# Two-layer attention with expert layers on one core: x kept on chip between the layers, expert outputs written by plain indirect writes, routing steps moved by an iteration or two

## The reference, cut to what matters

```python
x = x + tanh(g_xattn[0]) * attention_0(layernorm(x), ctx, mask)      # 64 x 64 tokens of 128, 16 heads of 8
x = x + tanh(g_ffn[0])   * experts_0(layernorm(x))                   # 8 experts, hidden 512, gelu, top 1
x = x + tanh(g_xattn[1]) * attention_1(layernorm(x), ctx)
x = x + tanh(g_ffn[1])   * experts_1(layernorm(x))                   # 16 experts, hidden 64, silu, top 2, capacity 8
```

## Time and profile before

| | us |
|---|---|
| median of 3 runs (lowest to highest) | 517.33 (516.51 to 517.77) |
| the profiled execution | 514.45 |
| its span, first to last instruction | 512.4 |
| PE busy | 443.6 |
| DVE busy | 349.9 |
| ACT busy | 320.6 |
| POOL busy | 272.6 |

### The profile page before, as it was taken

The page is one execution under the profiler, slowest core; times in us unless marked ns, Lnnn a source line. Parts: engine busy times, 40 slices in busy tenths (PEclk is TensorE's granted clock), DMA queues, the critical chain, the costliest instruction groups (busy, mean ns, idle before and its releaser), DMA issues.

```text
span 512.4 us, 21949 instructions
## 1 busy us (share of the span) xinstructions
PE 443.6 (87%) x8481; PEld 324.1 (63%) x8481; DVE 349.9 (68%) x883; ACT 320.6 (63%) x764; POOL 272.6 (53%) x325
## 2 busy tenths in 40 slices
PE   2789999999988796999998799998998697779996
PEld 1456676666655685999973466666665565445554
DVE  5578778888768665545532678888898677644545
ACT  2355566666865873677744466777777377685653
POOL 2622634646466178888886445553545236534454
PEclk9999999999999998999999799999999899898999
DMA  7124444232111155565436000110031000000112
GB/s 209 51 55 130 98 127 125 82 95 70 44 55 35 35 139 90 82 89 71 44 35 155 2 25 24 45 35 24 4 95 26 21 4 3 2 2 5 42 53 68
DMA packets 50629, 30.69 MB, mean 60 GB/s; under 512 B 12384, under 2 KB 46944, under 8 KB 50528
## 3 DMA queue, kind: packets, MB, share of 16 engines
q1 hardware_dynamic: 37072, 18.54, 13.7%
q0 software_dynamic: 6640, 4.67, 7.2%
q10 hardware_dynamic: 6816, 6.08, 4.3%
HBM read 19.42 MB, written 9.85 MB: 57 GB/s over the span
## 4 chain that ended last, share of the span: by engine, by line
PE 49%; DVE 20%; issue 13%; ACT 7%; POOL 4%; DMA 3%; ACTq 1%; DVEq 1%; SPq 0%; POOLq 0%
PE T_ps L865 8%; DVE maxes L600 7%; PE S_ps L854 6%; DVE prob L608 4%; PE A_ps L880 4%; PE f_H_ps L1199 3%; PE m_H_ps L1458 3%; PE f_Y_ps L1213 3%; PE S_ps L848 3%; PE Q_ps L835 2%; PE m_X_ps L1485 2%; PE m_T_ps L1498 2%; PE Q_ps L747 2%; PE m_X_ps L1469 2%; PE X_ps L897 2%
## 5 line engine op out<-in xcount | busy, mean ns | idle before, releaser
L600 DVE TENSOR_REDUCE maxes<-S_ps 128x16 f32<-128x1024 f32 x64 | 78.2, 1222 | 49.1 <-PE S_ps L854 49.0
L428 POOL TENSOR_TENSOR k_blk<-kT,col_a 128x512 f32<-128x512 f32 x64 | 67.7, 1067 | 79.4 <-ACT kT L489 54.0
L531 ACT ACTIVATE probT<-T_ps 128x512 f32<-128x512 f32 x128 | 76.0, 594 | 46.4 <-PE T_ps L865 45.6
L865 PE MATMUL T_ps<-col_a,prob 128*128 128x128 f32 x512 | 83.8, 287 | 15.1 <-DVE prob L608 11.3
L865 PEld LDWEIGHTS T_ps<-col_a,prob 128*128 128x128 f32 x512 | 56.5, 143 | 55.4 <-issue 29.9
L608 DVE TENSOR_TENSOR prob<-S_ps,maxes 128x512 f32<-128x512 f32 x128 | 82.5, 686 | 2.2
L1147 POOL DMA_INDIRECT x_mid<-f_out,f_rows x39 | 60.9, 1562 | 11.9 <-issue 9.2
L880 PE MATMUL A_ps<-v_blk,probT 128*32 128x18 f32 x4096 | 48.8, 187 | 0.1
L1012 DVE TENSOR_TENSOR f_hid<-f_H_ps,f_b 128x512 f32<-128x512 f32 x39 | 27.0, 692 | 31.5 <-PE f_Y_ps L1213 28.1
L880 PEld LDWEIGHTS A_ps<-v_blk,probT 128*32 128x32 f32 x4096 | 42.2, 111 | 9.5 <-issue 8.7
L854 PE MATMUL S_ps<-k_blk,qT 32*64 32x256 f32 x1024 | 46.9, 410 | 0.9 <-ACT qT L525 0.3
(11 more groups left out here) (199 smaller groups left out, 868.5 us busy)
## 6 DMA issues: line engine op xcount, KB each, us to landing
f_w<-in_W ACTq DMA_DIRECT2D x16, 256.0 KB, 3.0
ctxT<-in_ctxT SPq DMA_DIRECT2D x12, 256.0 KB, 3.0
f_rows<-sorted_rows SPq DMA_DIRECT2D x39, 64.5 KB, 2.1
out<-m_final SPq DMA_DIRECT2D x32, 64.0 KB, 1.5
x_all<-in_x SPq DMA_DIRECT2D x6, 256.0 KB, 5.7
x_mid<-x_all SPq DMA_DIRECT2D x6, 256.0 KB, 3.1
x_all<-x_mid SPq DMA_DIRECT2D x6, 256.0 KB, 3.5
ctxT<-in_ctxT SPq DMA_DIRECT2D x8, 128.0 KB, 2.7
```

The source lines that it names most:

```text
L428: nc.gpsimd.tensor_tensor(k_blk[:, t % 2, :, :, :], kT[:, g.at(R), t - g.first, :].rearrange("p (b k) -> p b k", b=2).unsqueeze(2).to_broa ...
L531: nc.scalar.activation(probT[:, t % 2, 4 * h:4 * h + 4, :], T_ps[:, :, :], ACT.Exp, scale=SCALE).then_inc(probT_ready, 1)
L600: nc.vector.tensor_reduce(maxes[:, t % 2, :, :], S_all[:, :, 0:HQ * S].rearrange("p r (e k) -> p r e k", k=S), X, ALU.max).then_inc(max_re ...
L865: last = nc.tensor.transpose(T_ps[:, j, :], pair, ident[:, :])
```

## The change

It has four parts.

1. `x_all` is no longer stored in and loaded from DRAM. `keep`, the `kept` waits, SP's `load_x` of layer 1 and `all_sent` go. Expert outputs go into a DRAM tensor `y_mid` by plain indirect writes, not accumulating ones. POOL then adds them to `x_all` group by group with an accumulating DMA (`raise_x`): the first waits for all sends; the first two stand ahead of the `k_blk` of tiles 32 and 33, the others in POOL's list at head -13. `stat` of layer 1 waits for `y_in`. The row numbers (`ids`) are changed so that a partition's rows of a group lie side by side in `y_mid`.
2. `out` and `hid` get room of their own, and `hid` a ring of three.
3. Logits of groups 0 to 4 in each layer come an iteration later, and stand after the k projection in PE's and ACT's lists.
4. The steps behind them move too (`spaced`: groups 3 and 4 of layer 0 and group 5 of layer 1 by one more), in layer 1 `top` to one place, last tile +12 (before: +9 and +10 by unit), `assign` from 11 to 13, `rank_slots` and `keep_ranks` from 12 to 14, `slots` from 13 to 14, `gaps` and `raise_` by two; in layer 0 `choose`, `rank`, `rows` and `scatter` by one.

```diff
+        def spaced(skew, steady):
+            return lambda g: settled(skew, steady, short, later)(g) + (g.own in ((3, 4) if masked else (5,)))
...
-                from_ = dram["x"] if masked else r["x_mid"]
-                sp.dma_start(x_group(g), from_[dram_rows(g), :].rearrange("(u p) d -> p u d", p=P)).then_inc(x_in[g.at(4)], 16)
+                sp.dma_start(x_group(g), dram["x"][dram_rows(g), :].rearrange("(u p) d -> p u d", p=P)).then_inc(x_in[g.own % 4], 16)
...
-            def keep(g):
-                sp.wait_ge(y_added, g.i + 1)
-                sp.dma_start(r["x_mid"][dram_rows(g), :].rearrange("(u p) d -> p u d", p=P), x_group(g)).then_inc(kept[g.own >= FULL_GROUPS], 16)
...
-            steps = [(load_x, groups, head(-13)), (load_ctx, late, head(-12))]
+            steps = [(load_ctx, late, head(-12))]
             if masked:
-                steps += [(load_mask, groups, head(-11)), (keep, groups, tail(5))]
+                steps = [(load_x, groups, head(-13))] + steps + [(load_mask, groups, head(-11))]
...
+            def raise_x(g):
+                if g.own == 0:
+                    for k, s in enumerate(r["y_sent"]):
+                        pool.wait_ge(s, 16 * ((MAX_TILES - k + len(r["y_sent"]) - 1) // len(r["y_sent"])))
+                pool.wait_ge(ln_stats, units_to(g.i - 4))
+                pool.dma_start(x_all[:, g.local * D:(g.local + g.n) * D],
+                               r["y_mid"][0:B * S, :].rearrange("(p t) d -> p (t d)", p=P)[:, g.local * D:(g.local + g.n) * D],
+                               accum_op=ALU.add).then_inc(y_in[g.own % 4], 16)
...
         def gpsimd_ahead(pool):
+            blocks, raise_x = gpsimd_steps(pool)
+            for g in groups[:2]:
+                raise_x(g)
             for t in tiles[:2]:
-                gpsimd_steps(pool)(t)
+                blocks(t)
...
-                steps += [(gaps, groups, settled(7, 11, short, later))]
+                steps += [(gaps, groups, settled(7, 13, short, later)), (raise_x, groups[2:], head(-13))]
...
-                dve.wait_ge(x_in[g.at(4)], 16 * (g.i // 4 + 1))
+                dve.wait_ge((x_in if masked else y_in)[g.own % 4], 16 * (g.own // 4 + 1))
...
-                steps += [(choose, groups, settled(6, 11, short, later)), (rows, groups, settled(7, 12, short, later)), (mask, groups, head(-4))]
+                steps += [(choose, groups, spaced(6, 12)), (rows, groups, spaced(7, 13)), (mask, groups, head(-4))]
             else:
-                steps += [(slots, groups, settled(9, 13, short, later)),
-                          (top, units, lambda u: u.group.last + 9 + u.k if u.group.own < short else settled(6, 9, short, later)(u.group)),
-                          (assign, groups, settled(7, 11, short, later)),
+                steps += [(slots, groups, spaced(9, 14)),
+                          (top, units, lambda u: settled(6, 12, short, later)(u.group)),
+                          (assign, groups, spaced(7, 13)),
...
-                     (rank if masked else rank_slots, groups, settled(7 if masked else 8, 12, short, later)), (attend, tiles, shift(1)), (logit, groups[:7], settled(6, 9, short, later)),
+                     (rank if masked else rank_slots, groups, spaced(7, 13) if masked else spaced(8, 14)), (attend, tiles, shift(1)), (logit, groups[apart:7], settled(6, 9, short, later)),
...
-                     (project_v, late_units, unit_head(-1)), (project_k, late, head(-3)),
+                     (project_v, late_units, unit_head(-1)), (project_k, late, head(-3)), (logit, groups[:apart], spaced(6, 10)),
...
-            wait(dve, y_ready, t - 1)
-            vec.tensor_tensor(hid[:, t % 2, :, :], H_ps[t % 2][:, :, :],
+            wait(dve, y_ready, t - HIDS + 1)
+            vec.tensor_tensor(hid[:, t % HIDS, :, :], H_ps[t % 2][:, :, :],
...
-            pool.indirect_dma_start(r["x_mid"], bass.IndirectOffsetOnAxis(ap=rows[:, t % RINGS, D:RW].bitcast(I32), axis=0),
-                                    out[:, t % DEEP, :], None, compute_op=ALU.add).then_inc(sent[t % DEEP], 16)
+            pool.indirect_dma_start(r["y_mid"], bass.IndirectOffsetOnAxis(ap=rows[:, t % RINGS, D:RW].bitcast(I32), axis=0),
+                                    out[:, t % DEEP, :], None).then_inc(sent[t % DEEP], 16)
```

More of the change, by code:

```diff
@@ L253, in attention @@
     x_in = [sem(f"x_in{k}") for k in range(4)]
+    y_in = [sem(f"y_in{k}") for k in range(4)]
     ctx_loaded = [sem(f"ctx_loaded{k}") for k in range(CR)]
     mask_loaded = [sem(f"mask_loaded{k}") for k in range(R)]
-    kept = [sem("kept_full"), sem("kept_rest")]
     mask_made = sem("mask_made")
@@ L472, in gaps @@
                 nc.gpsimd.tensor_tensor(r["gap"][:, at], r["top"][:, at, 1], r["top"][:, at, 0], ALU.subtract).then_inc(gap_ready, 1)
-            blocks = gpsimd_steps(pool)
+            blocks, raise_x = gpsimd_steps(pool)
             steps = [(blocks, tiles if masked else tiles[2:], shift(-2)), (norm, groups, head(-10)), (r_norm, groups, settled(3, 6, short, later))]
             if masked:
-                steps += [(scatter, tiles, lambda t: settled(8 if GROUP_OF[t].own < 7 else 7, 13, short, later)(GROUP_OF[t]) + (t - GROUP_OF[t].first) // (1 if GROUP_OF[t].own < LAST_GROUPS else 2))]
+                steps += [(scatter, tiles, lambda t: spaced(8 if GROUP_OF[t].own < 7 else 7, 14)(GROUP_OF[t]) + (t - GROUP_OF[t].first) // (1 if GROUP_OF[t].own < LAST_GROUPS - 1 else 2))]
             else:
-                steps += [(gaps, groups, settled(7, 11, short, later))]
+                steps += [(gaps, groups, settled(7, 13, short, later)), (raise_x, groups[2:], head(-13))]
             steps += [(add_bias, groups, head(-4))]
@@ L587, in scalar @@
             k_out, v_out = scalar_steps(act)
-            steps = [(exp(1), tiles, shift(0)), (keep_ranks, groups, settled(7 if masked else 8, 12, short, later)), (keep_logits, groups, settled(6, 9, short, later)), (avT_out, groups, tail(2)), (q_out, groups, head(-2)),
-                     (v_out, late_units, unit_head(-1)), (k_out, late, head(-3)),
+            steps = [(exp(1), tiles, shift(0)), (keep_ranks, groups, spaced(7, 13) if masked else spaced(8, 14)), (keep_logits, groups[apart:], settled(6, 9, short, later)), (avT_out, groups, tail(2)), (q_out, groups, head(-2)),
+                     (v_out, late_units, unit_head(-1)), (k_out, late, head(-3)), (keep_logits, groups[:apart], spaced(6, 10)),
                      (exp(0), tiles, shift(-1)), (r_xnT_out, groups, settled(5, 8, short, later)), (xnT_out, groups, turn_x_at), (normed, tiles, normed_at), (r_normed, units, lambda u: settled(4, 7, short, later)(u.group))]
             if not masked:
-                steps += [(raise_, groups[:SINGLY], tail(12)), (raise_last, [None], lambda _: RAISE_AT)]
+                steps += [(raise_, groups[:SINGLY], lambda g: g.last + (14 if g.own < short else 12)), (raise_last, [None], lambda _: RAISE_AT)]
             run(hook["first_scalar"](act) + steps + hook["scalar"](act))
@@ L920, in experts0 @@
     DEEP = 4
+    HIDS = 3
     def sb(name, shape, dt=F32):
@@ L952, in experts0 @@
     w1_now = sb("w1_now", [P, 2, HID0])
-    out = r["over_x"].take("f0_out", [P, DEEP, D])
-    hid = r["over_x"].take("f0_hid", [P, 2, NC0, P])
+    out = sb("out", [P, DEEP, D])
+    hid = sb("hid", [P, HIDS, NC0, P])
     H_ps = [ps(f"H_ps{n}", [P, NC0, P]) for n in range(2)]
@@ L977, in experts0 @@
     y_out = sem("y_out")
-    sent = [sem(f"sent{k}") for k in range(DEEP)]
+    sent = r["y_sent"]
+    assert len(sent) == DEEP
     vec, act, pe = nc.vector, nc.scalar, nc.tensor
@@ L998, in staggered @@
                     step(n - skew)
-    def all_sent(eng):
-        for k in range(DEEP):
-            eng.wait_ge(sent[k], 16 * ((MAX_TILES - k + DEEP - 1) // DEEP))
     def tile_vector(dve):
@@ L1134, in sync @@
             step(t)
-        all_sent(sp)
     def tile_gpsimd(pool):
         def send(t):
-            if t == 0:
-                pool.wait_ge(done["kept"][0], 16 * FULL_GROUPS)
-            if t == FULL_TILES:
-                pool.wait_ge(done["kept"][1], 16 * (NG - FULL_GROUPS))
             pool.wait_ge(y_out, t + 1)
@@ L1212, in down @@
             for n in range(NC0):
-                last = pe.matmul(Y_ps[t % 2][:, 0:D], hid[:, t % 2, n, :],
+                last = pe.matmul(Y_ps[t % 2][:, 0:D], hid[:, t % HIDS, n, :],
                                  w2[:, bass.ds(e, 1), n, :].rearrange("p a c -> p (a c)"),
```

21 lines of the change are left out of this document (10 added, 11 removed).

## The result

The changed kernel takes 528.4 us (median of 4 runs, 528.1 to 529.9), the kernel before 516.9 in the same series: a ratio of 1.0229, 95% interval 1.0201 to 1.0257, that is 11.5 us slower. The forecast was 519.7 with a range from 512.8 to 525.5: the sign was right, the size was not. Every time and ratio leaves out the executions in a slower state that the chip falls into now and then.

A forecast was written before the change was run, and what follows sets the result against it. PE was taken as the bound in the expert layer and nearly so in layer 1. Layer 1 starting 5.4 us later, less 3.0 from routing, gave 2.4 slower: 517.33 to 519.7 us, range 512.8 to 525.5.

The forecast's parts named there:

- The sends: Expert layer: plain sends cost POOL 0.99 us, not 1.555, and land after 3.0; the last lands 4.0 us earlier, third buffer included.
- the half that was the sign: End of expert layer: the last send would start within half a microsecond of the last `finish`.
- the 0.63: End of expert layer: the third `hid` buffer removes the last `down`'s wait for its gelu, 0.63 us.
- `raise_x`: Between the layers: loads moved into POOL's list make three landings follow one another, so layer 1 starts 5.4 us later.
- the three waits of `stat`: Start of layer 1, a sign: DVE waits in `stat` for `x_all` three times and not once.
- its 5.4: Start of layer 1: 5.4 us later in sum, the expert layer's 4.0 included; 0.8 to 9.8 by the bounds.
- The estimate of 2.6 us: Raise landing for 256 KB by the skill's rule, giving 3.0 in place of 5.4; set aside for the trace's 3.8.
- The routing of layer 0: Layer 0 attention: moved steps free PE's waits for DVE, 1.1 and 0.8 us, part of 3.0 gained over both layers.
- bounds of 0 and 5.3: Routing in both layers: gain from 0, each wait replaced by another, to 5.3 us with PE's waits for ACT.
- The sign that the wait for `r_chosen` goes: Layer 0 attention: PE's wait for `r_chosen`, 0.8 us before, would be gone.
- The routing of layer 1: Layer 1 attention: PE's waits for `both` and the subtractions, 1.0 and 0.9 us, mostly freed, within the 3.0 gain.
- routing gives nothing: Rival, both attentions: PE is nearly full and the waits come back elsewhere; 522.7 us, chance 0.15.

The follow-up runs named there:

- Early raises: The changed kernel with four raises, not two, issued ahead of the first `k_blk`: 520.0 us, ratio 1.0097 to the kernel before.
- scatters only: The changed kernel with layer 0 in the order of before, except POOL's scatters, which stay as changed: 526.8 us, ratio 1.0229 to the kernel before.
- logits in place: The changed kernel with the logits of groups 3 and 4 of layer 0 back in their old place: 526.7 us, ratio 1.0234 to the kernel before.
- four mends: The changed kernel, layer 0: old logit places, group 4 not delayed, its scatters single, group 2's paired; also four raises early: 515.6 us, ratio 1.0012 to before.
- Old layer 0: The changed kernel with the order of before in layer 0 alone: 523.2 us, ratio 1.0151 to the kernel before.
- old routing: The changed kernel with the routing places of parts 3 and 4 put back in both layers: 524.0 us, ratio 1.0151 to the kernel before.
- mends, old layer 1: The kernel of four mends with layer 1 in the order of before on PE, DVE and ACT: 514.8 us, ratio 1.0008 to the kernel before.
- routing only: The kernel before with only the new routing places, in both layers: 519.6 us, ratio 1.0063 to the kernel before.
- shift later: The kernel of mends, old layer 1 with layer 1's fourth-group `norm_shift` behind the first maxima on DVE: 517.1 us, ratio 1.0061 to the kernel before.

## Why the prediction was wrong

**The sends: right in the main.** 0.957 us of POOL each (0.99 forecast), landed after 2.4 (3.0). The last one starts 0.85 us after the last `finish` is done, and not within the half that was the sign: the last two `finish` start 1.06 us apart, and a send with its gap takes 1.26. From the start of the last `finish` to the landing of the last send, which is when POOL's wait for it ends (275.34 in the chain), it takes 3.9 us (forecast 3.6, before 7.0). The wait of the last `down` for its gelu is gone too, but the 0.63 are not in the time: the stage from tile 31 to the last `finish` takes 98.2 us, not less than 97.8.

**`raise_x`: mechanism right, size a little small.** The order in POOL's list, the three waits of `stat` and what ends them came as written. POOL's part is 0.91 (1.0 forecast), the landings 4.79, 4.16 and 4.27 (3.4 and twice 3.8), and the first raise is issued 0.55 us after POOL's wait ends (0.13). From the last landed send to the first maxima it is 20.4 us, forecast 19.5, before 10.1. Counted from the last `finish`, layer 1 starts 7.2 us later where the working has 6.0, its 5.4 without the 0.63 of the third buffer. Early raises shows that this is the serial order: it gives 6.7 of the 7.2 back. The estimate of 2.6 us for a 256 KB DMA by the Trainium skill (DMA: Bandwidth & Descriptors, Anatomy of one DMA — SWDGE (gpsimd) path) does not fit these landings of 4.2 in the median, though a plain send of 64 KB, 2.15 by the same estimate, lands after 2.2 to 2.9.

**The routing of layer 0: the step that failed.** The working took 3.0 us of gain and bounds of 0 and 5.3, both on the side of a gain. It costed which waits of PE would go, and not what the moved steps run into: it has no line for the scatters at all, which part 4 of the change moves, and none for a `choose` in the same iteration as a `logit` that has moved to its end. The sign that the wait for `r_chosen` goes failed with it: 0.8 us became 1.6. Steps 12 to 21 do gain, 0.6 us. Against that stand 2.4 us at step 22 (`choose` waits for late logits, then for `k_blk`), 2.1 at 26 and 1.0 at 29 (`k_blk` behind a second scatter, which scatters only puts at 1.4 and 1.0). Scatters only and logits in place show the two apart. With both taken away, in four mends, the maxima 12 to 31 take 92.0 us (before 92.3, changed 98.3), so there is no third.

**The routing of layer 1: no gain, the rival.** The wait for `both` went, as forecast, and the others came back as waits for ACT. Old layer 0 against old routing (both 1.0151) and four mends against mends, old layer 1 (1.0012 and 1.0008) give its worth as nothing that can be measured, the second pair to within some 2.6 us. The share of the 3.0 that was put there is the rival's "routing gives nothing".

**The sum.** With the sizes of these two traces: 7.2 between the layers, 5.5 - 0.6 in layer 0, 0 in layer 1, 12.1 against a measured 11.5. Forecast were 5.4 - 3.0 = 2.4. The miss is 7.9 of routing (4.9 + 3.0) and 1.8 of `raise_x` (7.2 - 5.4). That 12.1 comes so near to 11.5 is in part luck: it leaves out step 23, layer 1 and the end, 3.7 us more in the same traces, and by the ratios of whole runs routing costs less than 4.9: 4.0 us by old routing and by old layer 0, 3.3 by routing only.

**Left open.** Routing only is some 3 us faster than the steps of its profile make it. And steps of the same order differ between runs: step 17 takes 5.11 us before, and 6.7 to 8.1 in the five runs that have x on chip with the old order of layer 0, where PE stands still for 1.96 to 2.23 us (0.64 before) between two of the 32 products of one `logit`, for no semaphore that the profile shows. In all five a transfer on the queue that the profile calls instruction (q8) begins 0.3 to 0.5 us ahead of the stop and lands 1.4 to 1.5 us ahead of its end. PE waiting for its own instructions is thus a candidate; the runs without the stop have such a transfer near that place too, and it was not tried. The end is open as well: from the start of the last `m_final`, DVE's last operation on a tile, to the end of the span it is 3.6 us before and 3.0 in routing only, and 4.3 to 4.9 in each of the twelve kernels with x on chip. The prediction has no term for it, and no run shows its reason.

## What to carry to other kernels

A DMA that moves from an idle queue into the ordered list of a working engine takes that list's order with it: write the list out, and count how many landings now follow each other. When an instruction is moved by an iteration, cost what it meets in the new one on every engine that issues part of it, POOL's scatters too, and give the term a bound on the side of loss. A wait removed from one engine is worth nothing until the next one in line (here ACT for DVE) has been looked up. And look at the duration of a short DVE instruction, not only at the idle time ahead of it: here waits of up to 3.9 us stood inside it.

## What the runs showed of the hardware

Short DVE instructions with two inputs in SBUF wait for POOL's `k_blk`. Of the 60 in layer 0's routing in the trace of the changed kernel (`r_same`, `r_level`, `r_chosen`, `r_place`, `r_picked` and the running count; median 0.18 us) six took 0.85 to 1.78, and each of the six ended 0.03 to 0.06 us after a `k_blk`. The 19 that overlapped only the issue of an indirect DMA took no longer than usual, nor did three that lay wholly inside a 1.0 us `r_rstd` of POOL (128x4). Three of the six began 0.46 to 0.66 us ahead of their `k_blk`, during the issue of a scatter right before it; what held them already then is not shown. The timeline of step 26 in the changed kernel:

```profile
146.17 0.74 POOL L461 TENSOR_TENSOR x_all<-x_all,row_constants 128x256 f32<-128x256 f32 x1
...
146.41 1.55 DVE L675 TENSOR_TENSOR r_same<-l_logits,r_most 128x32 f32<-128x32 f32 x1
...
146.85 1.06 POOL L427 TENSOR_TENSOR k_blk<-kT,col_a 128x512 f32<-128x512 f32 x1
```

The Trainium skill (SBUF — State Buffer, SBUF: two separate sides) says that GpSimd shares one pair of ports with VectorE when that has two SBUF inputs and GpSimd's operation reads SBUF, as an exclusive lock that goes to whichever starts first, for its whole instruction. For `k_blk` the trace agrees in kind; it does not for `r_rstd`, nor for the three that began ahead of the `k_blk`. And it adds that DVE can lose the lock several times running: `r_same` came while POOL added the bias, and went on only after the `k_blk` behind it, and the `norm_shift` of shift later stood for 3.92 us through the issue of a raise, a `k_blk`, an `add_bias` and a second `k_blk`.

Accumulating direct DMAs into SBUF take POOL 0.91 us to issue. Their landing depends little on their size: 3.9 us in the median for 128 KB and 4.2 for 256 KB, 1.2 and 0.7 more than the loads of SP that they replace.
